# Sixteen batches written out without a loop, with a new order of the steps, in an attention and gate kernel

## The chip, the cores and the metric

The kernel runs on one core of one Trainium2 chip. The metric is the device time of one execution, in microseconds (us). It is stated as the median of several runs; beside it stands one profiled execution, from which every row below comes.

## The reference

For each of 16 batches of 512 tokens with 256 features, two networks read the same normalised tokens, and their product is added to the input:

```python
xn = _layernorm(x)
s = attention(xn)        # "talking heads": 16 heads of 16
g = silu(ffn(xn))        # 2 layers of local attention and a gated feed-forward
return x + s * g

# attention, per batch
logits = einsum(q, k) * SCALE
logits = einsum('bhij,gh->bgij', logits, Wpre)    # mix the heads before the softmax
attn = softmax(logits)
attn = einsum('bhij,gh->bgij', attn, Wpost)       # and after it
out = einsum(attn, v) @ Wout.T + bout

# one of the two layers of ffn, per batch
q, k, v = split(shift_token(x) @ wqkv)            # 8 heads of 64, l2norm, rotary, window 128
x = x + local_attention(q, k, v) @ wo
h = layernorm(shift_token(x)) * lg + lb
a, g = split(h @ w1 + b1)                         # 682 hidden columns each
x = x + (a * gelu(g)) @ w2 + b2
```

All of it is float32. Several products split each operand into a high and a low part and add three products of the parts.

## The kernel before

The work of a batch is cut into 351 steps, named by what they do and by their indices, and every engine goes through the same list and does its own part of each step.

The attention with mixed heads ("talk") has 64 tiles of 8 query rows by 16 heads, which makes 128 rows. `expand` on POOL spreads the queries with the mixing weights (`q_mix`), `part` splits them (ACT makes `q_hi`, POOL `q_lo`), `scores` multiplies on PE, takes the maximum on DVE and the exponential on ACT, and prepares `mixer_n` on DVE. `mix` multiplies `probs` by `mixer_n`, and DVE and ACT take turns at copying its bank M away. After each 8 tiles `values` multiplies by the values in pieces of 32 columns, and after each 16 `project` gives 128 tokens of output.

The gate network ("feed") goes, for each of its two layers, through `x_turn`, 4 windows of `qkv`, `join`, `q_turn` and `k_turn`, then 8 units of `local_scores` (64 rows deep), `weigh`, `p_turn` and `local_values` (64 columns), `out_proj`, then `half_turn`, `shift_turn`, `h_scale`, `h_turn`, 6 chunks of `up` (each with a Gelu on ACT) and 4 of `down`.

`AHEAD` are the steps that prepare the next batch's attention (`norm`, `scale`, `x_turn` 0, `talk_q`, `talk_k`, `talk_v`); they stand late in the list and work on batch b + 1. `BEHIND` are those that finish batch b - 1 (`bound`, four `sigmoid`, `silu`, `gated`, `store`); they stand early in the list. A `sigmoid` is an addition and a reciprocal on DVE.

The place of each step comes from three lists of numbers (`GATE_AT`, `FEED_AT`, `BEHIND_AT`): after how many steps of the talk part it stands. The resulting order is the same for each batch. `Counts.run` writes batch 0 out, then writes one body inside `eng.Fori(1, B)` that each engine repeats 15 times, and then writes `BEHIND` once more for the last batch:

```python
go(AHEAD, 0, True, early=True)
go(order, 0, True)
with eng.Fori(1, B) as b:
    go(order, b, False)
go(BEHIND, B, False)
```

Since the body is one for all, the last pass through it also loads a 17th batch (`x_next` is the input with batch 0 once more behind it) and does `AHEAD` for it, and the weights for a next batch are loaded once more.

`hidden` has 6 chunks of hidden columns; 682 columns leave 42 for the last. `down` multiplies the last chunk with 42 rows (L805):

```python
m = hidden_rows(i)
last = mm(bank[k][:, 0:D], hidden[0:m, i, t * P:(t + 1) * P], w_2[0:m, i, :], ...)
```

`w_2` holds zeros behind its 682nd row. Banks S0, S1, M, V and F0 to F3 are the eight of PSUM; a filling of a bank waits until its last one was emptied.

Of the kernel before, what the change touches and what calls it, by code (L numbers as in the profile page):

```python
# [14 lines left out]
P = 128  # L15
# [9 lines left out]
CT = 8  # L25
# [25 lines left out]
def hidden_rows(c):  # L51
    return min(P, HID - c * P)


# [5 lines left out]
def talk_steps():  # L60

    steps = []
    for n in range(TILES):
        steps.append(("scores", n))
        if n % CT == LAG and n >= CT:
            steps.append(("values", n // CT - 1))
        if n >= LAG:
            steps.append(("mix", n - LAG))
        if n % (2 * CT) == 5 and n >= CT:
            steps.append(("project", n // (2 * CT) - 1))  # L70
    assert LAG == 2
    return steps + [("mix", TILES - 2), ("talk_q",), ("mix", TILES - 1), ("talk_k",), ("values", CHUNKS - 1), ("talk_v",),
                    ("project", TW - 1)]


def feed_steps():

    steps = [("expand", 0)]
    for c in range(TILES // ET):
        steps += [("part", c), ("expand", c + 1)]  # L80
    return steps[:-1]


def gate_steps():

# [33 lines left out]
GATE_AT = [  # L119
# [6 lines left out]
]  # L126
FEED_AT = [
# [49 lines left out]
def gate_network_kernel(nc, a, out):  # L177

    order = step_order()

    filling, fillings = {}, {k: 0 for k in BANKS}
    for step in order:
        for k in banks_of(step):
            fillings[k] += 1
            filling[step, k] = fillings[k]

    early, ahead = {}, {k: 0 for k in BANKS}
    for step in AHEAD:
        for k in banks_of(step):
            ahead[k] += 1  # L190
            early[step, k] = ahead[k]

    with ExitStack() as ctx:
# [118 lines left out]
        filled = {k: sem(f"filled_{k}", fillings[k]) for k in BANKS}  # L312
        emptied = {k: sem(f"emptied_{k}", fillings[k]) for k in BANKS}
# [80 lines left out]
        class Counts:  # L394
# [24 lines left out]
            def run(self, eng, steps):

                def go(list_of_steps, b, first, early=False):
                    for step in list_of_steps:
                        if step[0] not in steps or step in BEHIND and first:
                            continue

                        self.b, self.first = (b + 1, False) if step in AHEAD and not early else (b, first)
                        steps[step[0]](step, *step[1:])
                        self.b, self.first = b, first
                go(AHEAD, 0, True, early=True)
                go(order, 0, True)  # L430
# [1118 lines left out]
```

## Time and profile before

| what | value |
| --- | --- |
| median of 3 runs | 5783.68 us (5781.62 to 5785.23) |
| the profiled execution | 5776.03 us, of which the span from the first to the last instruction is 5774.5 us |
| PE busy | 5549.4 us, 96% of the span |
| DVE busy | 3780.9 us, 65% |
| ACT busy | 2649.4 us, 46% |
| POOL busy | 2645.7 us, 46% |
| mean granted PE clock | 0.986 |

A busy PE means that a matmul was under way. Matmuls overlap, and so the distance from one start to the next says what one costs. Where rows below give a gap before an instruction, it stands in brackets, with what ended it; "issue" stands for a gap in which the engine waited for nothing that the profile shows. The granted clock is a share of the full one, 2.4 GHz; 0.5 is 1.2 GHz.

### The profile page before, as it was taken

The numbers are of one execution on the slowest core, as the hardware profiler recorded it, in microseconds if no ns is written. First come the engines' busy times: TensorE is split into PE (matmuls) and PEld (weight loads), VectorE is DVE, ScalarE is ACT, GpSimd is POOL, SyncE is SP. The second block draws the span as 40 slices with busy tenths as digits, with TensorE's granted clock in tenths as the row PEclk, the third lists the DMA queues.
The fourth block names the chain that finished last, engine by engine and source line by source line (L and its number), as shares of the span: only waits on it lengthen the run. The fifth ranks groups of instructions, "written<-read, shape, count | busy, mean of one in ns | idle before, by whom it ended". The sixth has DMA issues, their size and how long they took to land.

```text
span 5774.5 us, 138883 instructions
## 1 busy us (share of the span) xinstructions
PE 5549.4 (96%) x48336; PEld 4599.6 (80%) x48336; DVE 3780.9 (65%) x9938; ACT 2649.4 (46%) x6527; POOL 2645.7 (46%) x2315
## 2 busy tenths in 40 slices
PE   7999999999999999999999999999999999999998
PEld 5888878788787887878878788787877878778786
DVE  6666766666766667666676666766667676566665
ACT  4444544345443454534445344454444544445443
POOL 4344444444544445444354444544444444445443
PEclk9999999999999999999999999999999999999999
DMA  2211111111101111011110110101111111111111
GB/s 73 88 61 63 37 35 56 42 63 37 60 32 56 49 42 58 28 56 49 47 54 28 56 60 36 53 28 57 59 42 58 39 39 56 42 58 43 35 56 45
DMA packets 52185, 285.49 MB, mean 49 GB/s; under 512 B 5377, under 2 KB 22785, under 8 KB 34177
## 3 DMA queue, kind: packets, MB, share of 16 engines
q1 hardware_dynamic: 40560, 258.59, 12.1%
q0 software_dynamic: 10896, 17.30, 1.6%
q8 instruction: 443, 7.26, 0.5%
q14 instruction: 286, 2.33, 0.1%
HBM read 255.43 MB, written 28.84 MB: 49 GB/s over the span
## 4 chain that ended last, share of the span: by engine, by line
PE 87%; issue 5%; DVE 5%; ACT 1%; POOL 1%; DVEq 0%; SPq 0%; DMA 0%; ACTq 0%; POOLq 0%
PE bank_M L621 15%; PE bank_S L611 8%; PE bank_S L613 7%; PE bank_S L612 7%; PE bank_F L805 6%; PE bank_F L561 5%; PE bank_F L562 5%; PE bank_F L563 5%; PE bank_V L637 4%; PE bank_F L694 4%; PE bank_V L725 4%; PE bank_F L737 4%; PE bank_F L709 4%; PE bank_V L644 2%; PE bank_S L561 1%
## 5 line engine op out<-in xcount | busy, mean ns | idle before, releaser
L1388 POOL TENSOR_TENSOR q_lo<-q_mix,q_hi 128x512 fp32r<-128x512 f32 x512 | 684.4, 1337 | 1613.9 <-ACT q_hi L869 1613.7
L879 ACT ACTIVATE probs<-bank_S,neg_max 128x512 f32<-128x512 f32 x1024 | 701.9, 685 | 1260.5 <-DVE neg_max L1109 1258.6
L621 PEld LDWEIGHTS bank_M<-mixer_n,probs 128*128 128x128 f32 x8192 | 1048.2, 193 | 188.6 <-issue 109.8
L621 PE MATMUL bank_M<-mixer_n,probs 128*128 128x128 f32 x8192 | 1118.2, 280 | 63.7 <-ACT mixed L455 48.4
L1109 DVE TENSOR_REDUCE neg_max<-bank_S 128x1 f32<-128x512 f32 x1024 | 702.3, 686 | 567.2 <-PE bank_S L613 564.1
L611 PE MATMUL bank_S<-k_hi,q_lo 128*128 128x512 f32 x2048 | 898.4, 439 | 5.5 <-POOL q_lo L1388 5.5
L613 PE MATMUL bank_S<-k_hi,q_hi 128*128 128x512 f32 x2048 | 809.6, 395 | 0.0
L612 PE MATMUL bank_S<-k_lo,q_hi 128*128 128x512 f32 x2048 | 808.0, 395 | 0.0
L1382 POOL TENSOR_TENSOR q_mix<-q_rope,w_pre 128x256 f32<-128x256 f32 x1024 | 644.0, 657 | 57.6 <-POOL q_rope L1371 2.4
L932 ACT ACTIVATE l_probs<-l_probs,l_least 128x256 f32<-128x256 f32 (+1 forms) x1024 | 480.5, 471 | 264.4 <-DVE l_least L1198 264.3
L1414 POOL TENSOR_TENSOR l_probs<-l_probs,l_inv 128x1024 f32<-128x1024 f32 (+1 forms) x256 | 430.1, 1680 | 327.2 <-DVE l_inv L1218 327.2
L1399 POOL TENSOR_TENSOR inv_norms<-norms_c,minus_half 128x16 f32<-128x16 f32 x128 | 371.4, 2901 | 381.9 <-DVE norms_c L1152 381.9
L1198 DVE CUSTOM_DVE_ANT_0 l_probs<-bank_F,mask,inv_norms 128x256 f32<-128x256 f32 (+1 forms) x1024 | 401.9, 446 | 133.0 <-issue 131.6
L611 PEld LDWEIGHTS bank_S<-k_hi,q_lo 128*128 128x128 f32 x2048 | 389.5, 190 | 109.1 <-issue 51.1
L613 PEld LDWEIGHTS bank_S<-k_hi,q_hi 128*128 128x128 f32 x2048 | 387.2, 189 | 90.2
L1100 DVE TENSOR_SCALAR mixer_n<-mixer,row_inv 128x128 f32<-128x128 f32 x1024 | 424.1, 414 | 52.7
L869 ACT ACTIVATE q_hi<-q_mix 128x512 fp32r<-128x512 f32 x512 | 320.7, 626 | 264.6 <-POOL q_mix L1382 264.6
L612 PEld LDWEIGHTS bank_S<-k_lo,q_hi 128*128 128x128 f32 x2048 | 391.1, 191 | 50.7
L455 DVE COPY mixed<-bank_M 128x512 f32<-128x512 f32 x512 | 350.3, 684 | 100.5 <-PE bank_M L621 97.7
L1138 DVE TENSOR_TENSOR shared<-bank_F,rot 128x512 f32<-128x512 f32 x512 | 321.9, 683 | 113.9 <-PE bank_F L563 106.4
L805 PE MATMUL bank_F<-w,att 128*128 128x256 f32 (+1 forms) x1536 | 380.7, 392 | 0.0
L1297 DVE SCALAR_TENSOR_TENSOR att<-bank_F,b,shared 128x512 f32<-128x512 f32 x192 | 143.8, 749 | 339.3 <-ACT shared L984 329.0
(143 smaller groups left out, 10210.9 us busy)
## 6 DMA issues: line engine op xcount, KB each, us to landing
w_qkv_hi<-split_qkv SPq DMA_DIRECT2D x31, 1536.0 KB, 6.9
w_qkv_lo<-split_qkv SPq DMA_DIRECT2D x31, 1536.0 KB, 6.6
w_hi<-split SPq DMA_DIRECT2D x31, 1408.0 KB, 6.0
w_lo<-split SPq DMA_DIRECT2D x30, 1408.0 KB, 7.0
w<-in_w SPq DMA_DIRECT2D x33, 768.0 KB, 4.3
w_o<-in_w_o SPq DMA_DIRECT2D x33, 512.0 KB, 5.3
x_in<-in_x_next POOLq DMA_DIRECT2D x17, 512.0 KB, 3.9
out_y<-in_x_next SPq DMA_DIRECT2D x16, 512.0 KB, 7.5
```

Source lines behind the costliest of these rows:

```text
L611: mm(bank[k][:], q_lo[q], k_hi[:, s, :], start=(s == 0), stop=False)
L612: mm(bank[k][:], q_hi[q], k_lo[:, s, :], start=False, stop=False)
L613: last = mm(bank[k][:], q_hi[q], k_hi[:, s, :], start=False, stop=(s == 1))
L621: last = mm(bank["M"][:, j * P:(j + 1) * P], probs[:, n % PB, j * P:(j + 1) * P], mixer_n[:, n % 2, :], start=True, stop=True)
L805: last = mm(bank[k][:, 0:D], hidden[0:m, i, t * P:(t + 1) * P], w_2[0:m, i, :], start=(i == 0), stop=(i == HC - 1))
L879: fn(probs[:, n % PB, :], bank[k][:], ACT.Exp, bias=neg_max[:, n % 2:n % 2 + 1], accum_out=row_sum[:, n % PB:n % PB + 1]).then_inc(emptied ...
L932: fn(l_probs[:, u % LB, j, lo:], l_probs[:, u % LB, j, lo:], ACT.Exp, scale=-1.0, bias=l_least[:, u % 2, j:j + 1], accum_out=l_sum[:, u % ...
L1100: v.tensor_scalar(mixer_n[:, n % 2, :], mixer[:].rearrange("p g i -> p (g i)"), row_inv[:, n % 2:n % 2 + 1], None, ALU.mult).then_inc(mixe ...
L1109: v.tensor_reduce(neg_max[:, n % 2:n % 2 + 1], bank[k][:], AX.X, ALU.max, negate=True)\
L1382: g.tensor_tensor(q_mix[:, s].rearrange("p m (g i) -> p m g i", g=GH), q[:, :, None, :].to_broadcast(shape), w_pre[:, None, :, None].to_br ...
L1388: g.tensor_tensor(q_lo[:, c % QB], q_mix[:], q_hi[:, c % QB].bitcast(F32), ALU.subtract)\
L1414: g.tensor_tensor(l_probs[:, u % LB, :, lo:], l_probs[:, u % LB, :, lo:], l_inv[:, u % 2, :, None].to_broadcast([P, 4, 2 * P - lo]), ALU.m ...
```

## The change

The loop is gone. A function `program()` gives the list of all steps of all batches, each with its batch, and every engine's code is written out from it. Batch 0, the batches 1 to 14 and batch 15 have an order each, which are written out as text, step by step; a step still names the same work, except that `join` and `weigh` now also have their own places against their neighbours. The last order has no `AHEAD`, and its own `BEHIND` steps (`end.`) inside it. Loads of a batch or weights that nobody would use are left out. The waits on banks count fillings through the whole program. `project` also waits until ACT has copied the `values` before it. `down` multiplies 128 rows of the last chunk, and `up` writes 64 rows of it instead of 42 (its other rows meet zeros of `w_2`).

```diff
+ORDER = """
+expand.0 part.0 expand.1 bound qkv.0.0 join.0.0 scores.0 part.1 expand.2 qkv.0.1 scores.1 scores.2 join.0.1 part.2
+q_turn.0.0 expand.3 k_turn.0.0 mix.0 qkv.0.2 scores.3 mix.1 part.3 k_turn.0.1 q_turn.0.1 join.0.2 scores.4 scores.5
+expand.4 mix.2 part.4 qkv.0.3 mix.3 k_turn.0.2 scores.6 mix.4 join.0.3 expand.5 q_turn.0.2 scores.7 scores.8 mix.5
+q_turn.0.3 k_turn.0.3 mix.6 sigmoid.0 part.5 scores.9 mix.7 local_scores.0.0 scores.10 weigh.0.0 scores.11 mix.8
+expand.6 part.6 expand.7 local_scores.0.1 sigmoid.1 part.7 values.0 weigh.0.1 p_turn.0.0 mix.9 local_scores.0.2
+scores.12 expand.8 weigh.0.2 local_values.0.0 mix.10 p_turn.0.1 sigmoid.2 part.8 expand.9 scores.13 mix.11 sigmoid.3
...
+expand.31 scores.57 scores.58 values.6 mix.56 h_scale.1 scores.59 part.31 mix.57 h_turn.1 scores.60 scores.61 norm
+mix.58 up.1.0 scores.62 scale mix.59 up.1.1 up.1.2 mix.60 scores.63 x_turn.0 mix.61 up.1.3 up.1.4 mix.62 up.1.5 mix.63
+talk_q talk_k values.7 down.1.0 down.1.1 talk_v down.1.2 down.1.3 project.3
+"""
...
+LAST_ORDER = """
...
+up.0.1 part.17 mix.27 up.0.2 expand.18 up.0.3 up.0.4 up.0.5 scores.30 mix.28 scores.31 down.0.0 part.18 expand.19
...
+scores.60 mix.58 up.1.0 up.1.1 mix.59 up.1.2 up.1.3 part.31 up.1.4 up.1.5 end.silu scores.61 scores.62 down.1.0
+down.1.1 down.1.2 down.1.3 end.bound scores.63 end.gated end.sigmoid.0 end.store mix.60 mix.61 mix.62 end.sigmoid.1
+mix.63 end.sigmoid.2 values.7 end.sigmoid.3 project.3
+"""
...
+def program():
+
+    end = [("end", *step) for step in BEHIND]
...
+    steps = [(step, 0) for step in AHEAD]
+    for b in range(B - 1):
+        steps += [(step, b + (step in AHEAD)) for step in (step_order() if b else first_order()) if b or step not in BEHIND]
+    return steps + [(step[1:], B) if step[0] == "end" else (step, B - 1) for step in last_order()]
...
             def run(self, eng, steps):
...
-                go(AHEAD, 0, True, early=True)
-                go(order, 0, True)
-                with eng.Fori(1, B) as b:
-                    go(order, b, False)
-                go(BEHIND, B, False)
+                for step, b in steps_of_all:
+                    if step[0] in steps:
+                        self.b, self.first = b, b == 0
                         steps[step[0]](step, *step[1:])
...
             def qkv(step, l, t):
-                if t == TW - 1 and (l or not now.first):
+                if t == TW - 1 and (l or not now.first) and not last(l):
...
             def project(step, t):
                 pe.wait_ge(emptied["V"], now.fill(step, "V") - 1)
+                pe.wait_ge(emptied["V"], now.fill(("values", 2 * t + 1), "V"))
...
                 for i in range(HC):
-                    m = hidden_rows(i)
-                    last = mm(bank[k][:, 0:D], hidden[0:m, i, t * P:(t + 1) * P], w_2[0:m, i, :],
+                    last = mm(bank[k][:, 0:D], hidden[:, i, t * P:(t + 1) * P], w_2[:, i, :],
                               start=(i == 0), stop=(i == HC - 1))
...
-                m, b = hidden_rows(i), BLOCKS - 1 if i == HC - 1 else i
+                m, b = (TAIL_G, BLOCKS - 1) if i == HC - 1 else (P, i)
...
-                if not l:
-
-                    pool.dma_start(x_in[:], a["x_next"][bass.ds(now.b + 1, 1)].rearrange("a p t f -> (a p) t f"))\
-                        .then_inc(x_loaded, 16)
+                if not l and now.b < B - 1:
+
+                    pool.dma_start(x_in[:], a["x"][now.b + 1]).then_inc(x_loaded, 16)
```

## Rows read from the trace of the kernel before

**Rows 1.** The page, part 1: busy time, share of the span, instructions.

```profile
PE 5549.4 (96%) x48336; PEld 4599.6 (80%) x48336; DVE 3780.9 (65%) x9938; ACT 2649.4 (46%) x6527; POOL 2645.7 (46%) x2315
```

**Rows 2.** Waits of PE: total us, times, longest.

```profile
PE bank_M L621 <- ACT mixed L455: 48.4, 15, 3.2
...
PE bank_F L562 <- issue: 28.8, 14, 2.3
PE bank_F L561 <- issue: 27.3, 14, 2.5
```

**Rows 3.** Stretches: the start of the program, and its end behind PE; busy per engine, granted clock.

```profile
0.00:45.00 45.00, 12.42 (x56) 10.49 (x57) 14.74 (x34) 9.57 (x10) 6.68 (x9) 1.00 0.65 232
...
5751.00:5774.50 23.50, 0.00 (x0) 0.00 (x0) 8.86 (x10) 1.06 (x1) 6.03 (x3) 0.61 0.17 22
```

**Rows 4.** Timeline of PE from batch 0 into the first pass.

```profile
416.97 1.89 PE L644 MATMUL bank_V<-w_out,oT 128*128 128x256 f32 x8
...
422.83 0.39 PE L611 MATMUL bank_S<-k_hi,q_lo 128*128 128x512 f32 x1
```

**Rows 5.** Timeline of PE from the sixth pass into the seventh.

```profile
2543.87 1.89 PE L644 MATMUL bank_V<-w_out,oT 128*128 128x256 f32 x8
2547.83 0.79 PE L561 MATMUL bank_F<-w_qkv_hi,xT_hi 128*128 128x512 f32 x1 [2.08 <-issue]
...
2556.36 0.39 PE L611 MATMUL bank_S<-k_hi,q_lo 128*128 128x512 f32 x1
```

**Rows 6.** Stretches: a place in the seventh pass, and the way into it; columns as above.

```profile
2589.90:2599.00 9.10, 5.88 (x23) 4.88 (x24) 7.44 (x21) 3.07 (x9) 3.00 (x4) 0.62 0.00 1
2544.70:2557.80 13.10, 9.01 (x30) 6.79 (x30) 4.38 (x8) 2.31 (x4) 4.07 (x6) 0.74 0.02 6
```

**Rows 7.** Timeline of PE and its weight loads in the last batch.

```profile
5740.18 6.03 PE L805 MATMUL bank_F<-w,att 128*128 128x256 f32 x24
...
5742.53 0.29 PEld L805 LDWEIGHTS bank_F<-w,att 42*128 42x128 f32 x2 [0.33 <-issue]
...
5746.14 0.39 PE L561 MATMUL bank_S<-w_v_hi,xT_hi 128*128 128x256 f32 x1
...
5749.09 1.89 PE L644 MATMUL bank_V<-w_out,oT 128*128 128x256 f32 x8
```

**Rows 8.** Groups of instructions of PE and POOL: busy us, mean ns of one, idle before.

```profile
L644 PE MATMUL bank_V<-w_out,oT 128*128 128x256 f32 x512 | 121.0, 379 | 0.0
...
L1399 POOL TENSOR_TENSOR inv_norms<-norms_c,minus_half 128x16 f32<-128x16 f32 x128 | 371.4, 2901 | 381.9 <-DVE norms_c L1152 381.9
```

**Rows 9.** Timeline of PE: the `scores` right behind a `local_scores`.

```profile
2604.15 0.50 PE L611 MATMUL bank_S<-k_hi,q_lo 128*128 128x512 f32 x1
2604.49 0.40 PE L612 MATMUL bank_S<-k_lo,q_hi 128*128 128x512 f32 x1
```

**Rows 10.** Timeline of DVE, then of PE, in the seventh pass.

```profile
2587.46 1.75 DVE L1322 RECIPROCAL x_mid<-x_mid 128x256 f32<-128x256 f32 x1
...
2589.39 1.75 DVE L1322 RECIPROCAL x_mid<-x_mid 128x256 f32<-128x256 f32 x1
2591.06 0.63 DVE L1109 TENSOR_REDUCE neg_max<-bank_S 128x1 f32<-128x512 f32 x1
...
2593.12 2.05 PE L621 MATMUL bank_M<-mixer_n,probs 128*128 128x128 f32 x8 [3.23 <-ACT mixed L455]
```

**Rows 11.** Timeline of PE at the same place in the second pass.

```profile
815.18 1.13 PE L621 MATMUL bank_M<-mixer_n,probs 128*128 128x128 f32 x8 [3.23 <-ACT mixed L455]
...
821.21 0.72 PE L694 MATMUL bank_F<-att 64*128 64x128 f32 x8 [1.78 <-DVE l_least L1198]
```

**Rows 12.** Timeline of ACT in the last batch.

```profile
5740.31 0.39 ACT L895 ACTIVATE oT<-bank_V 128x256 f32<-128x256 f32 x1 [4.05 <-PE bank_V L637]
5740.72 1.28 ACT L989 ACT_TABLE_LOAD   x1
```

**Rows 13.** Timeline of DVE and POOL behind PE's last matmul.

```profile
5751.48 0.69 DVE L1315 TENSOR_SCALAR x_mid<-x_tok 128x1024 f32<-128x1024 f32 x1
...
5766.38 1.35 POOL L1442 DMA_DIRECT2D out_y<-s_tok  x1 [0.30 <-POOL s_tok L1437]
```

**Rows 14.** Timeline of PE: one `values`.

```profile
406.13 1.99 PE L637 MATMUL bank_V<-mixed,v_heads 128*32 128x64 f32 x128
```

More of the change, by code:

```diff
@@ L60, in talk_steps, with value_steps @@
 def talk_steps():
+    assert LAG == 2
     steps = []
[L63 to L73, printed above, removed]
+    for n in range(TILES + LAG):
+        steps += [("scores", n)] * (n < TILES) + [("mix", n - LAG)] * (n >= LAG)
+    return steps
+def value_steps():
+    steps = []
+    for c in range(CHUNKS):
+        steps += [("values", c)] + [("project", c // 2)] * (c % 2)
+    return steps
 def feed_steps():
@@ L81, in feed_steps, with join_steps @@
     return steps[:-1]
+def join_steps():
+    steps = []
+    for l in range(LAYERS):
+        steps += [("join", l, t) for t in range(TW)] + [("weigh", l, u) for u in range(TW * QUADS)]
+    return steps
 def gate_steps():
@@ new lines @@
+x_turn.1 mix.31 scores.33 part.18 qkv.1.0 values.3 join.1.0 qkv.1.1 k_turn.1.0 join.1.1 expand.19 q_turn.1.0 mix.32
+scores.34 scores.35 qkv.1.2 k_turn.1.1 q_turn.1.1 part.19 expand.20 mix.33 join.1.2 qkv.1.3 mix.34 scores.36 join.1.3
+q_turn.1.2 part.20 k_turn.1.2 scores.37 scores.38 q_turn.1.3 mix.35 k_turn.1.3 scores.39 expand.21 mix.36
+local_scores.1.0 project.1 weigh.1.0 mix.37 part.21 scores.40 expand.22 mix.38 part.22 p_turn.1.0 local_scores.1.1
+scores.41 expand.23 mix.39 part.23 weigh.1.1 local_values.1.0 local_scores.1.2 scores.42 values.4 local_scores.1.3
@@ new lines @@
+"""
+FIRST_ORDER = """
+expand.0 part.0 expand.1 qkv.0.0 join.0.0 part.1 scores.0 expand.2 qkv.0.1 join.0.1 scores.1 k_turn.0.0 part.2
+q_turn.0.0 expand.3 qkv.0.2 mix.0 scores.2 k_turn.0.1 join.0.2 bound scores.3 part.3 expand.4 q_turn.0.1 mix.1 qkv.0.3
+mix.2 scores.4 scores.5 silu q_turn.0.2 k_turn.0.2 part.4 sigmoid.0 mix.3 join.0.3 expand.5 scores.6 mix.4 scores.7
+k_turn.0.3 q_turn.0.3 sigmoid.1 part.5 mix.5 local_scores.0.0 mix.6 scores.8 local_scores.0.1 expand.6 part.6 scores.9
+mix.7 weigh.0.0 scores.10 local_scores.0.2 values.0 p_turn.0.0 weigh.0.1 mix.8 scores.11 expand.7 weigh.0.2
@@ new lines @@
+x_turn.1 mix.31 part.19 scores.33 qkv.1.0 values.3 join.1.0 qkv.1.1 k_turn.1.0 mix.32 q_turn.1.0 expand.20 join.1.1
+scores.34 qkv.1.2 mix.33 part.20 join.1.2 store q_turn.1.1 expand.21 k_turn.1.1 scores.35 qkv.1.3 sigmoid.3 mix.34
+scores.36 join.1.3 k_turn.1.2 q_turn.1.2 part.21 scores.37 scores.38 expand.22 q_turn.1.3 mix.35 k_turn.1.3 scores.39
+mix.36 local_scores.1.0 part.22 project.1 weigh.1.0 mix.37 scores.40 mix.38 local_scores.1.1 scores.41 expand.23
+mix.39 p_turn.1.0 weigh.1.1 local_scores.1.2 part.23 values.4 mix.40 scores.42 scores.43 p_turn.1.1 weigh.1.2
@@ new lines @@
+part.28 mix.50 out_proj.1.2 local_values.1.6 p_turn.1.7 expand.29 mix.51 local_values.1.7 scores.53 part.29
+out_proj.1.3 scores.54 mix.52 scores.55 expand.30 part.30 expand.31 mix.53 half_turn.1 scores.56 mix.54 shift_turn.1
+project.2 mix.55 scores.57 scores.58 h_scale.1 values.6 mix.56 scores.59 mix.57 h_turn.1 scores.60 scores.61 norm
+mix.58 up.1.0 part.31 scale up.1.1 mix.59 up.1.2 mix.60 scores.62 scores.63 x_turn.0 mix.61 up.1.3 up.1.4 mix.62
+up.1.5 talk_q mix.63 talk_k down.1.0 talk_v down.1.1 down.1.2 values.7 down.1.3 project.3
@@ new lines @@
+down.0.1 down.0.2 down.0.3 mix.29 x_turn.1 mix.30 scores.32 scores.33 mix.31 qkv.1.0 join.1.0 values.3 qkv.1.1
+k_turn.1.0 scores.34 join.1.1 part.19 mix.32 q_turn.1.0 qkv.1.2 mix.33 scores.35 scores.36 q_turn.1.1 join.1.2
+expand.20 mix.34 k_turn.1.1 part.20 qkv.1.3 mix.35 q_turn.1.2 scores.37 scores.38 k_turn.1.2 join.1.3 mix.36 scores.39
+scores.40 expand.21 mix.37 q_turn.1.3 k_turn.1.3 part.21 scores.41 mix.38 local_scores.1.0 project.1 expand.22 part.22
+mix.39 local_scores.1.1 weigh.1.0 expand.23 part.23 weigh.1.1 scores.42 mix.40 local_scores.1.2 values.4 scores.43
@@ L524, in up @@
                     spill_1(l)
-                if i == HC - 1 and (l or not now.first):
+                if i == HC - 1 and (l or not now.first) and not last(l):
                     k, = banks_of(step)
@@ L1543 @@
          for k, v in arrays.items()}
-    a["x"] = a["x_next"]
     out = nc.dram_tensor("out_y", (B, N, D), F32, kind="ExternalOutput").ap()
```

158 lines of the change are left out of this document (92 added, 66 removed), and 9 rows, old and new, of tables (FEED_AT, GATE_AT).

## Prediction

> **What bounds the kernel now.** The first thing to read is the busy share of each engine [rows 1]. PE works in 5549.4 of 5774.5 us, DVE in 65% of them, ACT and POOL in 46%. So PE sets the time, and a change is worth what it takes from PE: matmul time, gaps, or clock. PE is idle for 225.1 us in all. The second view is its waits, which say where [rows 2]: 56.1 us go to two gaps marked "issue" that come 14 times each, and 48.4 us to one `mix` that waits 15 times. The stretches give two more [rows 3]: 45.0 - 12.4 = 32.6 us before the first `qkv`, and 23.5 us behind the last matmul. What is left over is 225.1 - 56.1 - 48.4 - 32.6 - 23.5 = 64.5 us in small waits, 4.0 us a batch. The third view is the timeline of PE at those places, since a gap is followed by slow matmuls, and the distance between starts shows what busy time hides.
>
> **The loop's end.** Between batch 0 and the first pass nothing branches back: from the last `project` (416.97) to the first `scores` (422.83) PE needs 5.86 us [rows 4]. Between the sixth pass and the seventh the same instructions need 2556.36 - 2543.87 = 12.49 us, with a gap of 2.08 us that waits for nothing [rows 5]; the second gap is as long, 28.8/14 = 2.06 us [rows 2]. The other 2.6 us are clock: 0.74 was granted over that stretch, so for a time after the idle gaps PE runs at 1.2 instead of 2.4 GHz [rows 6]. The back edge thus costs 12.49 - 5.86 = 6.6 us here. The 14 back edges have 56.1 us of gaps, 4.0 each, against 4.1 here, and I take 6.4 each: **14 x 6.4 = 90 us**. If the clock came down for another reason and stayed down, the gaps alone, 56 us, would be gained; more than 93 (14 x 6.6) I cannot see.
>
> The crossing from batch 0 into the first pass is straight code and has no such gap. The Trainium skill ("Runtime: NRT & Kernel Launch", Instruction fetch mechanics) says the same: instructions are fetched ahead in sequence only, a taken branch to a far target must wait, and straight code hides its fetching. By that rule all 90 us go, and 15 times as many written-out instructions add no gap; the trace agrees as far as batch 0 shows it.
>
> **The last chunk of `down`.** Two `down` steps take 5746.14 - 5740.18 = 5.96 us, 2.98 each for 12 matmuls [rows 7]. Full-height matmuls of 256 columns lie (1.89 - 0.38) / 7 = 0.216 us apart: that is `project`'s row [rows 7], where a single one lasts 379 ns [rows 8]. Twelve of them are 2.59 us. The 0.39 us of difference lies at the 42-row loads, before which the load path stands idle for 0.33 us [rows 7]. With 128 rows no such edge is left, and rows cost no columns. There are 16 x 2 x 4 = 128 of these steps, all on PE's path: **128 x 0.39 = 50 us**. Where a `down` has a neighbour with another shape, one of its two edges stays; in the new orders no `down` is followed by `values` in batches 1 to 14, so I take off nothing. The 64 rows that `up` writes instead of 42 run side by side and cost nothing on DVE or ACT.
>
> **Fewer changes of shape.** The same edge stands wherever PE goes between full height and width and `local_scores` (64 rows), `local_values` (64 columns) or `values` (32 columns). Half of 0.39 is 0.2 us an edge; what can be seen outside the odd step alone is 0.34 - 0.23 = 0.11 us in the first distance behind `local_scores` [rows 9]. Counting neighbours in PE's order, the old body has 76 edges, the order of batches 1 to 14 has 69, the first 66 and the last 71. That is 14 x 7 + 10 + 5 = 113 edges: at 0.2 **23 us**, at 0.11 it would be 12.
>
> **The four sigmoids.** In each pass DVE does sigmoids 1 and 2 back to back. Its next maximum, at 2591.06, comes at least 3.6 us after 2587.46, and the `mix` that follows starts 3.23 us late [rows 10]. That is the 48.4 us in the waits (the waiting `mix` is put down to ACT, but ACT waits for DVE's maximum). Batch 0 has no sigmoids, and no such wait. In the seventh pass the clock then falls (0.62 over 9.1 us [rows 6]), and the eight matmuls that end the gap take 2.05 us instead of 1.13; in the second it stays up, but PE meets a next wait of 1.78 us 6 us later [rows 11]. So one pass loses 3.23 + 1.78 = 5.0 us, another 3.23 plus up to 2.7 of clock; I take 5.5. The new order sets `sigmoid.0` behind `mix.6`, `.1` behind the second `local_scores`, and the last two with a `scores` and a `mix` between them. I added up DVE's and PE's work along both lists. With the old one DVE falls 5.3 us behind PE at the first `local_scores`, with the new one never more than 3.5 in that part. Two tiles of PE's work (2 x 2.3 us) lie between a `scores` and its `mix`, and maximum, exponential and scaling need about 2, so a lag up to some 3 us is hidden. So the wait goes: **15 x 5.5 = 82 us**. Bounds: nothing, if the lag merely moves, and 88.
>
> **The other waits.** 4.0 us a batch. Some come from places that the new order changes (`mix.61` before `x_turn` 0, `scores.60`), and 1.4 us a batch would be a third of them: 15 x 1.4 = 21 us. Against it stands ACT: the old list changes between Exp and Gelu four times a batch, the new one eight times, since `scores.62` and `scores.63` stand among the `up` steps. Each change is a table load of 1.28 us, which starts as soon as the activation before it ends [rows 12]. ACT is busy 46%, so 14 x 4 x 1.28 = 72 us of work are hidden nearly everywhere. Where they might show is `up.1.4`, which needs the bank that ACT and DVE empty after `x_turn` 0: adding up from `up.1.0`, I find it 0.7 us late. 14 x 0.7 = 10 us. Together **10 us**, between -72 (all loads exposed) and +64 (no wait left).
>
> The Trainium skill ("ScalarE: Activation LUTs", What ACT_TABLE_LOAD costs) prices a change of table at about 2.66 us, of which a drain is half. The trace shows 1.28 and no drain in front of the load, and I go by the trace.
>
> **The last batch.** It has no `AHEAD`: `talk_q` and `talk_k` are 24 matmuls of 0.24 us (of the 5.86 us of [rows 4], 8 x 0.216 = 1.7 are `project`'s at most, and 18 matmuls of 512 columns share the other 4.2), 5.7 us, `x_turn` (8 of 0.11) 0.9. `talk_v` lay behind `down` and is counted in what follows. Now the end: the last `down` ends at 5746.14 [rows 7], and 28.4 us later all is over. In the new order `bound` follows it at once (0.7 us for the addition), the chain from `bound` to the end stays 5774.5 - 5751.48 = 23.0 us [rows 13], its last part being the store, 8.1 us. Up to 2.6 us of DVE's work for `scores.63` and two `mix` comes between the sigmoids: 26.3 instead of 28.4, 2 us gained. Under the chain lies now what PE did before it: `scores.63` 1.4 us, four `mix` of 0.9, `values` 1.9 [rows 14] = 6.9 us. Sum: 5.7 + 0.9 + 6.9 + 2 = **16 us**, between 9 (nothing hidden) and 19.
>
> Batch 0 keeps its waits for the splitting of the weights. The loads left out are off the path (DMA waits do not appear in rows 2). `join` and `weigh` move against their neighbours on POOL, priced under the rivals.
>
> **Sum.** 90 + 50 + 23 + 82 + 10 + 16 = 271 us. The profiled execution took 5776.0 us, so 5505 us. The median of the runs shown lies 7.7 us above that execution; 5505 + 7.7 gives **5513 us**, -4.7%.
>
> **Rivals.**
> 1. No wait is left in the batches: the 64.5 us of small waits go instead of 10. 5513 - 54 = 5459 us. For it: DVE, ACT and POOL have room. Against it: DVE still falls behind at times.
> 2. The reordering brings nothing: the lag of DVE moves elsewhere and makes an equal wait, so the 82 and the 10 fail. 5513 + 92 = 5605 us. For it: DVE's work in the first 60 us of a batch is the same (some 92% of PE's), and taking 6.4 us of stops out of PE gives it less time to catch up.
> 3. The table loads are exposed: 72 us instead of 10 hidden in the sum, 5513 + 62 = 5575 us. For it: `part` and `scores` wait for ACT in order. Against it: ACT's 46%.
> 4. Slower than before: POOL. In the new order `part.1` stands behind `join.0.0`, and so behind a power of 2.9 us [rows 8] that waits for all of `qkv.0.0` on DVE; the old list had three parts done before it. I get `q_lo` for `scores.2` 0.2 us before PE wants it. [...] To end on the other side this must cost 271/14 = 19 us in each batch, while only one power and one product (4 us) lie in front of it. 3 in 100.
>
> **Chances and range.** The sum 0.62, no waits left 0.12, reordering in vain 0.13, tables 0.08, slower 0.03, no change 0.02. The likeliest one's own range is 5470 to 5555: shape edges at 0.11 and 3 us of waits a batch more on one side, 3 us less on the other. The range that holds 8 in 10 is 5445 to 5590: it takes in the first and the third rival, and part of the second. Differences below 0.2% could not be told from none by a measurement of this kernel. Faster by more than that: 0.95; within: 0.02; slower: 0.03.
>
> **What would show it.** Right: PE's waits for "issue" are gone, and no matmul at 1.2 GHz is seen at batch starts; the 42-row form is gone and `down` steps are 2.59 us; the 3.2 us wait before a `mix` is gone; the batches are some 337 to 340 us apart, against 355.5 (5332 us for 15); ACT has about 60 more table loads; the mean granted clock is above 0.99. Wrong: a new wait that comes 14 times, above all at `scores` for `q_lo` or at `mix`; or gaps for "issue" spread over the straight code.

## The result, and the profile after

| | before | after |
| --- | --- | --- |
| median of 4 runs | 5782.65 us (5775.81 to 5785.23) | 5510.11 us (5509.82 to 5510.46) |
| profiled span | 5774.5 us | 5508.7 us |
| mean granted PE clock | 0.986 | 0.997 |

The ratio is 0.953, with a 95% interval of 0.9514 to 0.9547: the changed kernel takes 4.7% less. 5513 was predicted.

The page of the changed kernel, part 1, which answers to [rows 1]:

```profile
PE 5403.8 (98%) x48280; PEld 4601.9 (84%) x48280; DVE 3794.9 (69%) x9913; ACT 2710.1 (49%) x6581; POOL 2647.8 (48%) x2308
```

PE is idle for 104.9 us instead of 225.1, so 120 of the 266 us of span were gaps. The other 146 are busy time: 56 fewer matmuls, but above all matmuls that no longer run at 1.2 GHz, no longer stretch over a change of shape, and `down` without its odd chunk. Waits of PE (total us, times, longest), for [rows 2]:

```profile
PE bank_F L657 <- DVE x_in L1138: 32.1, 1, 32.1
PE bank_S L696 <- POOL q_lo L1473: 21.7, 16, 5.5
PE bank_V L811 <- ACT pT L1026: 8.7, 14, 0.9
PE bank_V L762 <- POOL shared L1491: 8.2, 17, 0.5
PE bank_M L706 <- ACT mixed L537: 7.5, 18, 1.6
...
PE bank_V L722 <- issue: 3.4, 8, 0.9
```

Both rows of 14 gaps for "issue" are gone, and so is the wait of 3.2 us before a `mix`. What is left at the top is the start of the program (once) and a wait of `scores` for `q_lo`: 5.5 us once in batch 0, which the kernel before had too, and new 16.0 us in the 14 steady batches, as batches 1 to 14 are called here. The last row is small, but it belongs to the signs that the prediction gave: `values`, which is 128 short matmuls, stops 8 times in its middle for "issue", where it did so 3 times for 0.8 us in all before. Stretches (busy time of each engine, granted clock), for [rows 3] and [rows 6]:

```profile
0.00:45.00 45.00, 11.41 (x53) 9.68 (x54) 14.38 (x34) 9.57 (x10) 6.33 (x9) 1.00 0.65 232
...
400.00:5160.00 4760.00, 4717.22 (x42339) 4019.94 (x42338) 3311.99 (x8665) 2365.83 (x5758) 2318.27 (x2021) 1.00 0.14 49
```

The clock is granted in full over the steady batches. The timeline of PE where one batch passes into the next, for [rows 5]:

```profile
2438.01 5.34 PE L890 MATMUL bank_F<-w,att 128*128 128x256 f32 x24
2443.19 1.89 PE L730 MATMUL bank_V<-w_out,oT 128*128 128x256 f32 x8
2444.73 0.58 PE L646 MATMUL bank_F<-w_qkv_hi,xT_hi 128*128 128x512 f32 x1
...
2449.00 0.39 PE L696 MATMUL bank_S<-k_hi,q_lo 128*128 128x512 f32 x1
```

From `project` to the first `scores` it now takes 2449.00 - 2443.19 = 5.81 us, as in batch 0 before [rows 4], and not 12.49. Two `down` steps take 5.18 us, 2.59 each, instead of 5.96 [rows 7]. From start to start the steady batches are 339.2 us apart, against 355.5.

### The profile page after: what moved, and what is told of

It is laid out like the page before. It is cut to its first block and busy times, and to the rows that moved or that the text cites. A ratio compares the mean times of both kernels' runs of the same rounds, so it can differ in the third digit from the quotient of the medians.

```text
span 5508.7 us, 130052 instructions
## 1 busy us (share of the span) xinstructions
PE 5403.8 (98%) x48280; PEld 4601.9 (84%) x48280; DVE 3794.9 (69%) x9913; ACT 2710.1 (49%) x6581; POOL 2647.8 (48%) x2308
## 5 line engine op out<-in xcount | busy, mean ns | idle before, releaser
L706 PE MATMUL bank_M<-mixer_n,probs 128*128 128x128 f32 x8192 | 1092.9, 276 | 12.8 <-ACT mixed L537 7.5
L696 PE MATMUL bank_S<-k_hi,q_lo 128*128 128x512 f32 x2048 | 877.4, 428 | 21.7 <-POOL q_lo L1473 21.7
L1484 POOL TENSOR_TENSOR inv_norms<-norms_c,minus_half 128x16 f32<-128x16 f32 x128 | 402.9, 3147 | 334.6 <-DVE norms_c L1237 332.8
L1185 DVE TENSOR_SCALAR mixer_n<-mixer,row_inv 128x128 f32<-128x128 f32 x1024 | 431.6, 421 | 169.0 <-PE bank_M L706 57.7
L537 ACT COPY mixed<-bank_M 128x512 f32<-128x512 f32 x512 | 296.9, 580 | 142.1 <-PE bank_M L706 83.1
```

The costliest lines, as they stand in the source:

```text
L537: copy(mixed[:, :, :, m * RI:(m + 1) * RI], bank["M"][:].rearrange("p (j g i) -> p j g i", j=TW, g=GH)).then_inc(emptied["M"], 1)
L696: mm(bank[k][:], q_lo[q], k_hi[:, s, :], start=(s == 0), stop=False)
L706: last = mm(bank["M"][:, j * P:(j + 1) * P], probs[:, n % PB, j * P:(j + 1) * P], mixer_n[:, n % 2, :], start=True, stop=True)
L1185: v.tensor_scalar(mixer_n[:, n % 2, :], mixer[:].rearrange("p g i -> p (g i)"), row_inv[:, n % 2:n % 2 + 1], None, ALU.mult).then_inc(mixe ...
```

## The experiments

Twelve kernels ran. Batch lengths are distances between first `qkv` matmuls, a mean over batches 1 to 14; the last batch runs from its first `qkv` matmul to the end. In the sets of runs below the kernel before had medians of 5775.7 to 5778.6 us, so spans and batch lengths compare better than differences of medians.

### The parts one by one

**a: whole rows alone.** In the kernel before, `down` takes 128 rows and `up` writes 64.

```diff
-                    m = hidden_rows(i)
-                    last = mm(bank[k][:, 0:D], hidden[0:m, i, t * P:(t + 1) * P], w_2[0:m, i, :],
+                    last = mm(bank[k][:, 0:D], hidden[:, i, t * P:(t + 1) * P], w_2[:, i, :],
```

> The kernel before (loop and old order), with the last chunk of down alone multiplied in 128 rows. Theory (each down loses 0.39 us at its 42-row matmuls, all on PE's path): 5783 - 50 = 5733 us, and down steps of 2.59 us instead of 2.98. Rival (the freed time is lost again in waits of the old order, since PE reaches them earlier): 5758 us or more, and longer waits of PE.

Measured: 5735.68 us, ratio 0.9929 (0.9912 to 0.9946), 40.0 us less; its span is 42.4 us shorter. A `down` step got 0.37 us shorter in the traces (2.93 to 2.56 in the mean), 48 us in all; the rest came back in waits: the two rows for "issue" grew from 56.1 to 60.2 us.

**b: no loop, and nothing else.** All three orders are the old list, the last one without `AHEAD`; `down` keeps its 42 rows.

```diff
-                with eng.Fori(1, B) as b:
-                    go(order, b, False)
+                for step, b in steps_of_all:
```

> The kernel after with the old order in every batch and 42 rows in down: the loop alone is gone, and with it the 17th AHEAD. Theory (a back edge costs 6.4 us of gap and low clock, 14 of them, and 10 us of PE work of the unneeded AHEAD): 5783 - 100 = 5683 us, no wait for issue, PE's clock up at the starts of batches. Rival 1 (gaps go, the clock stays down): 5717 us. Rival 2 (straight code is fetched no faster, the gaps spread over it): about 5770 us, with issue gaps at other places.

Measured: 5687.19 us, ratio 0.9844 (0.9828 to 0.9861), 88.5 us less. Neither row for "issue" of [rows 2] is there any more. The wait of the `mix` is, and larger: 54.3 us in 15 places instead of 48.4. The timeline of PE where batch 6 passes into batch 7, which answers to [rows 5]:

```profile
2522.18 1.89 PE L730 MATMUL bank_V<-w_out,oT 128*128 128x256 f32 x8
2523.71 0.58 PE L646 MATMUL bank_F<-w_qkv_hi,xT_hi 128*128 128x512 f32 x1
...
2528.04 0.39 PE L696 MATMUL bank_S<-k_hi,q_lo 128*128 128x512 f32 x1
```

These are 5.86 us, and so it is at every crossing of b, within 0.01. In the kernel before the 14 crossings take 9.76 to 13.34 us, 12.15 in the mean, and so b gains 88 us at the crossings alone. Its batches, however, are only 5.3 us shorter (355.6 to 350.25), 75 us in all; the last batch is 13.9 us shorter. The rest is not waits: without the two rows for "issue" PE is idle for 169.0 us before, and for 167.9 in b. It is clock. From the waiting `mix` to 12 us behind its start the granted clock was 1.00 in 4 of the 14 steady batches before, and 0.74 to 0.86 in the others; in b it is 0.73 to 0.86 in all 14. What the lower clock takes in the part around that `mix` (20 to 80 us into a batch) grows by that from 1.7 to 2.7 us a batch, as an estimate from the granted clock.

**c: b with whole rows**, so that only the new order is missing.

```diff
-                    last = mm(bank[k][:, 0:D], hidden[0:m, i, t * P:(t + 1) * P], w_2[0:m, i, :],
+                    last = mm(bank[k][:, 0:D], hidden[:, i, t * P:(t + 1) * P], w_2[:, i, :],
```

> As the kernel without the loop and with the old order, and 128 rows in down. Theory (the two parts add): 5633 us. What is then missing to the kernel after, 5510 us, is the new order: 123 us. Rival (they share a wait): 5645 us or more.

Measured: 5643.32 us, ratio 0.9767 (0.9751 to 0.9784), 132.4 us less; against 40.0 + 88.5 = 128.5 for the two alone, they add up. Its waits of PE, and the seventh batch's:

```profile
PE bank_M L706 <- ACT mixed L537: 54.4, 15, 3.6
PE bank_F L657 <- DVE x_in L1138: 40.9, 16, 31.2
PE bank_M L706 <- DVE mixed L537: 13.8, 31, 1.4
```

```profile
2546.24 1.13 PE L706 MATMUL bank_M<-mixer_n,probs 128*128 128x128 f32 x8 [3.63 <-ACT mixed L537]
```

So the order of the steps carries 5643.32 - 5510.11 = 133 us, half of the whole gain.

The straight code has gaps for "issue" of its own, at other places. In c PE stops in the middle of a `values`:

```profile
2258.63 1.86 PE L722 MATMUL bank_V<-mixed,v_heads 128*32 128x64 f32 x115
2262.44 0.42 PE L722 MATMUL bank_V<-mixed,v_heads 128*32 128x64 f32 x13 [1.95 <-issue]
```

There are five such gaps at `values` in b (5.7 us) and in c (7.1 us), and the eight in the changed kernel (3.4 us). That is b's second rival, but small: it expected some 5770 us. No run shows what these gaps wait for.

### Where the order's gain comes from

**d: the old order with its sigmoids spread out.** Against c, each `sigmoid` has other steps between itself and the next. All four also come later, and `silu` and `gated` move behind them:

```diff
-mix.1 part.3 expand.4 join.0.3 scores.4 sigmoid.0 mix.2 q_turn.0.3 scores.5 part.4 mix.3 sigmoid.1 sigmoid.2 expand.5
-scores.6 k_turn.0.3 mix.4 scores.7 part.5 mix.5 sigmoid.3 local_scores.0.0 scores.8 mix.6 local_scores.0.1 scores.9
+mix.1 part.3 expand.4 join.0.3 scores.4 mix.2 q_turn.0.3 scores.5 part.4 mix.3 expand.5 scores.6 k_turn.0.3 mix.4
+scores.7 part.5 mix.5 sigmoid.0 local_scores.0.0 scores.8 mix.6 local_scores.0.1 sigmoid.1 scores.9 expand.6 weigh.0.0
+mix.7 sigmoid.2 local_scores.0.2 weigh.0.1 scores.10 values.0 p_turn.0.0 mix.8 sigmoid.3 silu gated part.6
```

> As the last one, with the four sigmoids alone moved apart in the old order: behind mix.5, the second local_scores, mix.7 and mix.8, with silu and gated behind them. Theory (two sigmoids back to back make DVE 3.2 us late for a mix, and with what follows that costs 5.5 us in each of 15 batches): 5633 - 82 = 5551 us, and the 48 us wait of mix for ACT is gone. Rival (DVE's work is the same, its lag comes out at another step): about 5633 us, with a new wait that comes 15 times.

Measured: 5646.89 us, ratio 0.9778 (0.9762 to 0.9794): no gain over c. The waits of PE show where the time went:

```profile
PE bank_S L696 <- POOL q_lo L1473: 31.7, 16, 5.5
PE bank_F L780 <- DVE l_least L1283: 22.3, 29, 1.0
PE bank_V L811 <- ACT pT L1026: 20.5, 15, 1.4
```

The large wait at the `mix` is gone, and three others, 74.5 us, stand in its place (in c the first is 5.5, the second 2.5 us, and the third is not there). The expected 5551 us was missed, and the rival, the lag coming out at another step, held. Not all of it comes out at DVE itself. Before the 2.23 us wait for `q_lo` in batch 6, POOL does the two products of `gated`, which wait for the last sigmoid:

```profile
2209.43 2.39 POOL L1516 TENSOR_TENSOR x_mid<-x_mid,x_tok 128x1024 f32<-128x1024 f32 x1 [2.48 <-DVE x_mid L1407]
2211.96 2.35 POOL L1521 TENSOR_TENSOR s_tok<-s_tok,x_mid 128x1024 f32<-128x1024 f32 x1
2214.27 1.26 POOL L1473 TENSOR_TENSOR q_lo<-q_mix,q_hi 128x512 fp32r<-128x512 f32 x1
```

So this one way of spreading the sigmoids in the old order moves the wait; whether another would do better was not tried.

**e: the new order with its sigmoids squeezed together** as in the old list.

```diff
-expand.4 mix.2 part.4 qkv.0.3 mix.3 k_turn.0.2 scores.6 mix.4 join.0.3 expand.5 q_turn.0.2 scores.7 scores.8 mix.5
-q_turn.0.3 k_turn.0.3 mix.6 sigmoid.0 part.5 scores.9 mix.7 local_scores.0.0 scores.10 weigh.0.0 scores.11 mix.8
+expand.4 mix.2 part.4 qkv.0.3 mix.3 k_turn.0.2 scores.6 sigmoid.0 mix.4 sigmoid.1 sigmoid.2 join.0.3 expand.5
+q_turn.0.2 scores.7 scores.8 mix.5 q_turn.0.3 k_turn.0.3 mix.6 sigmoid.3 part.5 scores.9 mix.7 local_scores.0.0
```

> The kernel after with the sigmoids of batches 1 to 14 moved back early: behind scores.6, two together behind mix.4, the last behind mix.6. Theory (DVE has no slack there, two in a row make a maximum late): some 3 to 5 us a batch more, 5510 + 14 x 4 = 5566 us, with a wait of mix of 2 to 3 us, 14 times. Rival (the new order has slack enough elsewhere; the old wait came from something else): 5510 to 5520 us.

Measured: 5610.06 us, ratio 0.9713 (0.9698 to 0.9728), 100 us more than the changed kernel, 7.2 us a batch, where 3 to 5 were expected. The wait comes 14 times, as expected, but at a `q_turn` (L762) and not at a `mix`. The wait and the stretch around it:

```profile
PE bank_F L762 <- DVE shared L1251: 44.6, 14, 3.2
```

```profile
2526.00:2536.00 10.00, 8.20 (x40) 6.73 (x41) 7.98 (x17) 3.94 (x9) 3.49 (x4) 0.66 0.01 2
```

Over the 10 us around such a wait the granted clock is 0.66. Of the 100 us, 59 are idle time of PE (163.7 us instead of 104.8; 45 of them this wait, the rest waits that grew elsewhere), and 40 are busy time for the same number of matmuls (5443.5 instead of 5403.8 us). Of the two placements tried, neither was enough alone: the spread sigmoids in the old list, and the squeezed ones in the new.

**k and l: the sigmoids' work taken out**, in the old order (k, on c) and in the new one (l, on the changed kernel).

```diff
-                fn(x_mid[:], x_mid[:], ACT.Exp, scale=-1.0).then_inc(exp_done, 1)
+                fn(x_mid[:], x_mid[:], ACT.Copy, scale=-1.0).then_inc(exp_done, 1)
...
-                v.reciprocal(x_mid[:, t, :], x_mid[:, t, :]).then_inc(sig_done, 1)
+                v.reciprocal(x_mid[:, t, 0:1], x_mid[:, t, 0:1]).then_inc(sig_done, 1)
```

> The kernel without the loop and with whole rows in down, but with the old order of steps, in which each sigmoid's reciprocal covers one column instead of the whole tile and the exponential ahead of it is a plain copy (so the sigmoids' values are left out; about 1.6 us of VectorE work four times a batch is gone). Theory, that VectorE's lag behind the sigmoids is what costs 6.7 us a batch in the old order: 5643 less 15 x 6.7 = 100, about 5543 us, and the wait of the mixes for ScalarE (54 us in 15 places) gone. Rival, that the lag has another source: 5620 us or more, with that wait still there.

> The changed kernel with the same cut: each sigmoid's reciprocal covers one column, its exponential is a plain copy (the sigmoids' values are left out). Theory, that the new order already absorbs the sigmoids: within some 10 us of the changed kernel's 5510 us, 5495 to 5510. Rival, that the new order only spreads the sigmoids' price over many small waits: tens of us less, 5480 or below.

Measured: k 5563.57 us, ratio 0.9629 (0.9614 to 0.9644), 79.8 us less than c where 100 were expected; its batches went from 347.53 to 342.55 us, 5.0 each. The wait of the `mix` fell as k's row shows:

```profile
PE bank_M L706 <- ACT mixed L537: 9.3, 15, 0.6
```

l 5504.63 us, ratio 0.9529 (0.9514 to 0.9543), 5.5 us less than the changed kernel; its batches stay 339.2 us apart, so that in the steady batches of the new order the sigmoids cost nothing that can be seen. In the profiles the difference lies in batch 0, which has no sigmoids (5.3 us, scatter), and in the last batch (2.0). So the sigmoids cost 79.8 us in the old order and at most 5.5 in the new one: 74 of the 133 us or a little more. The other 59 stand between k and l, where no sigmoid plays a part: 14 x 3.35 = 47 in the steady batches (342.55 and 339.20 us), 12.6 in batch 0 (371.3 and 358.7), and under 2 in the last. The 14 steady batches of k, then of l:

```profile
414.55:5210.17 4795.62, 4740.45 (x42170) 3984.75 (x42169) 3239.81 (x8652) 2301.20 (x5698) 2321.16 (x2017) 1.00 0.14 49
```

```profile
403.20:5152.01 4748.81, 4706.29 (x42171) 4010.40 (x42169) 3223.57 (x8652) 2363.19 (x5754) 2312.57 (x2016) 1.00 0.14 49
```

The clock is the full one in both, and the matmuls are the same. PE's busy time falls by 34 us, so its matmuls lie closer together, and its idle time by 13.

### The table loads

**g: the `up` steps of layer 1 kept together**, `scores.62` and `scores.63` before them.

```diff
-mix.58 up.1.0 scores.62 scale mix.59 up.1.1 up.1.2 mix.60 scores.63 x_turn.0 mix.61 up.1.3 up.1.4 mix.62 up.1.5 mix.63
+mix.58 scale mix.59 scores.62 mix.60 scores.63 up.1.0 up.1.1 up.1.2 x_turn.0 mix.61 up.1.3 up.1.4 mix.62 up.1.5 mix.63
```

> The kernel after with scores.62 and scores.63 of batches 1 to 14 set before up.1.0, so that ACT changes its table 4 times a batch instead of 6 for the second layer's part (28 loads of 1.28 us less or more gone). Theory (the loads are hidden): the same within 0.3%, 5500 to 5525 us; all that can change is small waits from the closer row of scores and mix. Rival (exposed loads): 5510 - 14 x 2 x 2.6 = 5440 us.

Measured: 5593.33 us, ratio 0.9682 (0.9667 to 0.9697), 83 us more. Both expectations missed, although 56 loads are gone (69 instead of 125) and not 28. The waits of the `mix` for DVE and ACT grew to 30.7 and 30.3 us and `x_turn` now waits 24.2: from `mix.58` to `scores.63` no PE work of the feed part stands between the tiles any more. It suggests that the `up` steps are cover for the tiles; of the loads it tells nothing, since the edit moved both.

**h: four more loads in each steady batch**, behind the exponentials of `scores.62` and `scores.63`, and the order left alone.

```diff
+                if n >= TILES - 2 and 0 < now.b < B - 1:
+                    j = 4 * now.b + 2 * (n % 2)
+                    fn(spare[:, j:j + 1], b_qk[:, 0:1], ACT.Gelu)
+                    fn(spare[:, j + 1:j + 2], b_qk[:, 0:1], ACT.Exp)
```

> The changed kernel with four more table loads in each of batches 1 to 14 where the ups lie: a one-column Gelu and a one-column Exp on ScalarE behind the exponentials of scores.62 and of scores.63 (extra work, nothing left out); some 56 more loads of 1.28 us, 72 us of ScalarE in all, and about 0.9 us a batch of small instructions. Theory, that ScalarE has room there and the loads lie beside TensorE's work: 5510 to 5520 us. Rival, that table loads at the ups are exposed: up to 72 us more by the loads alone and 84 with the small instructions, 5580 to 5594 us.

Measured: 5540.57 us, ratio 0.9588 (0.9573 to 0.9603), 30.5 us more, between the two expectations. Two new waits of PE, 14 times each:

```profile
PE bank_F L647 <- DVE xT_lo L1150: 15.7, 14, 1.1
PE bank_F L658 <- DVE att L1387: 14.1, 14, 1.3
```

```profile
2423.30 1.28 ACT L969 ACT_TABLE_LOAD   x1
2424.59 0.20 ACT L969 ACTIVATE spare<-b_qk 128x1 f32<-128x1 f32 x1
2424.80 1.28 ACT L970 ACT_TABLE_LOAD   x1
2426.09 0.20 ACT L970 ACTIVATE spare<-b_qk 128x1 f32<-128x1 f32 x1
2426.20 1.06 ACT L932 ACTIVATE xT_hi<-bank_F 128x512 fp32r<-128x512 f32 x2
```

At each of the two places 3.0 us of ACT went in and about 1.1 us of PE came out. The changed kernel itself has no wait at `up.1.3` or `up.1.4`. So its own loads are hidden; the room left at each place is, as an estimate from these numbers, 3.0 - 1.1 = 1.9 us, and no more.

### The end, and the new wait

**i: the last batch in the steady order**, without `AHEAD`, its `end.` steps behind everything.

```diff
-expand.0 part.0 bound expand.1 qkv.0.0 scores.0 join.0.0 part.1 expand.2 scores.1 qkv.0.1 scores.2 q_turn.0.0 part.2
...
+down.1.1 down.1.2 down.1.3 project.3 end.bound end.sigmoid.0 end.sigmoid.1 end.sigmoid.2 end.sigmoid.3 end.silu
+end.gated end.store
```

> The kernel after, where the last batch has the order of the others without AHEAD, and its own BEHIND steps stand behind everything. Theory (the order of the last batch puts 6.9 us of PE's work under the chain of sigmoids and stores and lets bound start earlier): 6 to 9 us more, 5518 us. Rival (the end costs the same, since the chain is shared with DVE's other work): 5510 us.

Measured: 5511.32 us, ratio 0.9543 (0.953 to 0.9556), 1.2 us more, where 6 to 9 were expected; that is too little to be told from none. Within the profiled last batch it is 3.8 us (354.3 against 350.5). PE behind the last `down` steps, changed kernel:

```profile
5471.78 10.52 PE L890 MATMUL bank_F<-w,att 128*128 128x256 f32 x48
...
5486.14 1.13 PE L706 MATMUL bank_M<-mixer_n,probs 128*128 128x128 f32 x8 [1.57 <-ACT mixed L537]
5488.15 1.13 PE L706 MATMUL bank_M<-mixer_n,probs 128*128 128x128 f32 x8 [0.88 <-DVE mixed L537]
```

```profile
5483.07 0.69 DVE L1400 TENSOR_SCALAR x_mid<-x_tok 128x1024 f32<-128x1024 f32 x1 [0.30 <-DVE x_tok L1391]
...
5501.03 1.34 POOL L1526 DMA_DIRECT2D out_y<-s_tok  x1 [0.30 <-POOL s_tok L1521]
```

and in i:

```profile
5474.40 10.63 PE L890 MATMUL bank_F<-w,att 128*128 128x256 f32 x48
5484.86 1.89 PE L730 MATMUL bank_V<-w_out,oT 128*128 128x256 f32 x8
```

The last order moves its last `down` forward by 5.7 us within the batch, but the chain behind it takes 5508.7 - 5482.3 = 26.4 us against 5509.5 - 5485.0 = 24.5. DVE needs 10.9 us for the four sigmoids, with the `scores` and `mix` work between them, and 7.9 us in i, where they stand alone.

**f: `part.1` before `qkv.0.0`** in all three orders.

```diff
-expand.0 part.0 expand.1 bound qkv.0.0 join.0.0 scores.0 part.1 expand.2 qkv.0.1 scores.1 scores.2 join.0.1 part.2
+expand.0 part.0 expand.1 part.1 bound qkv.0.0 join.0.0 scores.0 expand.2 qkv.0.1 scores.1 scores.2 join.0.1 part.2
```

> The kernel after with part.1 set ahead of bound and qkv.0.0 in each order, so that POOL makes this q_lo before the power and the product of join. Theory (PE waits 1.14 us for it 14 times, and 5.5 us in batch 0 for the first): 14 x 1.1 = 16 us less, 5494 us. Rival (the wait passes on to the next q_lo or to a window of qkv that now comes later): 5505 to 5512 us.

Measured: 5489.54 us, ratio 0.9504 (0.9491 to 0.9517), 20.6 us less than the changed kernel, a little more than the 16 expected. The batches are 338.0 us apart, which is 17 us for the 14, and of the wait for `q_lo` only batch 0's is left:

```profile
PE bank_S L696 <- POOL q_lo L1473: 5.5, 1, 5.5
```

**m: f with four more steps moved**, each of which waits in every steady batch.

```diff
-q_turn.0.3 k_turn.0.3 mix.6 sigmoid.0 part.5 scores.9 mix.7 local_scores.0.0 scores.10 weigh.0.0 scores.11 mix.8
-expand.6 part.6 expand.7 local_scores.0.1 sigmoid.1 part.7 values.0 weigh.0.1 p_turn.0.0 mix.9 local_scores.0.2
-scores.12 expand.8 weigh.0.2 local_values.0.0 mix.10 p_turn.0.1 sigmoid.2 part.8 expand.9 scores.13 mix.11 sigmoid.3
+q_turn.0.3 mix.6 k_turn.0.3 sigmoid.0 part.5 scores.9 mix.7 local_scores.0.0 scores.10 weigh.0.0 scores.11 mix.8
+expand.6 part.6 expand.7 local_scores.0.1 sigmoid.1 part.7 values.0 weigh.0.1 mix.9 p_turn.0.0 local_scores.0.2
+scores.12 expand.8 weigh.0.2 mix.10 local_values.0.0 p_turn.0.1 sigmoid.2 part.8 expand.9 scores.13 mix.11 sigmoid.3
...
-x_turn.1 mix.31 scores.33 part.18 qkv.1.0 values.3 join.1.0 qkv.1.1 k_turn.1.0 join.1.1 expand.19 q_turn.1.0 mix.32
+x_turn.1 mix.31 scores.33 part.18 qkv.1.0 values.3 join.1.0 qkv.1.1 join.1.1 expand.19 q_turn.1.0 k_turn.1.0 mix.32
```

> The kernel in which the part of the local attention's norm on GpSimd is issued earlier (5489.5 us), with four more steps moved in batches 1 to 14: local_values.0.0 behind mix.10, p_turn.0.0 behind mix.9, k_turn.0.3 behind mix.6, k_turn.1.0 behind q_turn.1.0. These are the steps that wait longest in each steady batch, some 1.5 us together of what moving can reach. Theory, that each wait ends on work that is only issued too close: 14 x 1.5 = 21 us less, about 5469 us. Rival, that the waits pass on to the next step, since the engine named there is busy throughout: 5485 to 5492 us.

Measured: 5490.48 us, ratio 0.9502 (0.9489 to 0.9515), the same as f. Its waits:

```profile
PE bank_M L706 <- ACT mixed L537: 15.6, 18, 1.6
PE bank_M L706 <- DVE mixed L537: 10.0, 16, 0.9
PE bank_F L795 <- POOL l_probs L1499: 6.7, 14, 0.7
```

The wait for `pT` (8.7 us) is gone and that for POOL's `shared` fell from 7.9 to 1.3 us, but the two rows of the `mix` went from 7.4 and 3.9 us to 15.6 and 10.0, with 6.7 for `l_probs` beside them: 15 us out, 21 in. The rival, that the waits pass on to the next step, was right.

## Why the prediction was right, point by point

The time came out as forecast, and the experiments show each large term; the reason given for one of them, the order, was only half right. That the sum is within 3 us of the measurement is in part luck, since its errors point both ways.

- **Back edges (90 us), with the last batch's missing `AHEAD` (6.6 us in the sum; 10 with `talk_v`, as b's expectation has it).** b was expected to gain 100 us and gained 88.5. The mechanism is shown: the gaps and the slow clock go with the loop, and at the crossings themselves the term is right (88 us). No batch's start has a gap in the straight code. The Trainium skill's rule ("Runtime: NRT & Kernel Launch", Instruction fetch mechanics) says that straight code hides its fetching, and the trace agrees there; at `values` some gaps for "issue" remain, 3.4 us in the changed kernel. What went wrong is that the time gained at the crossings did not all reach the end: the 14 batches got 75 us shorter and not 88, since the clock now came down behind the waiting `mix` in every batch and not in ten of 14. The sum had no term for that.
- **`down` (50 us).** The steps themselves gave 48 us; 40 to 44 reached the end (a alone, and c against b), because part of what PE saves is waited for elsewhere.
- **The order (82 + 23 + 10, and 9 of the last batch's 16, together 124 us).** Measured 133. The largest term, the sigmoids, is 79.8 - 5.5 = 74 us, where 82 stood. The reason given was only half right. By the sum along the lists the new order would never let DVE fall over 3.5 us behind in that part; the lag itself was not measured, but no wait for it is left there. The reason named the sigmoids' spacing. d and e show that this spacing alone is not it: spread out in the old list they gain nothing, squeezed in the new one they cost 100 us. The second rival's mechanism was thus real for d, and not for the change.
- **Shapes, other waits and the last batch (42 us).** 59 us, of which 47 in the steady batches: 34 of busy time and 13 of waits, by the stretches of k and l. The sum had 14 x 7 edges x 0.2 = 20 us of shapes there, and so this term was too small, or the matmuls came closer for another reason as well. No experiment separates them. In the changed kernel a `scores` step takes 1.37 us at the shortest, 1.50 behind a `local_scores`, and 1.58 between a `local_scores` and a `values`, which speaks for 0.1 to 0.2 us a change. Batch 0 was said to keep its waits, but its order gained too: it takes 371.3 to 371.6 us in the three profiles with the old order and whole rows (c, d, k), and 358.7 to 364.0 in six with the new one (the changed kernel, e, g, h, i, l). The six run the same batch 0, and so single profiles scatter by 5 us there.
- **The last batch.** The chain behind the last `down` came out as forecast (26.3 said, 26.4 measured). What the forecast missed is that the plain end's chain would have been 24.5 and not the 28.4 of [rows 7], which still had `talk_v` in it: the last order brings 1 to 4 us, not 9.
- **Table loads (10 us lost at `up.1.4`).** There are 60 more, as forecast, 125 in all, and no wait at `up.1.4`. The third rival fell: h shows that even four more a batch cost 30.5 of 84 us.
- **POOL (the fourth rival).** Its place was right, its size small. `q_lo` for `scores.2` was to come 0.2 us early and came 1.14 us late, 14 times; f took it away and gained 20.6 us. Of the 1.34 us of error, 1.02 are a power that took 3.92 us instead of 2.90 (below).

The sum agrees better than its terms: 7 us of the total are the kernel before itself, whose median was 5782.65 us here and 5775.7 beside a, b and c. From there it is 88.5 + 43.9 + 133.2 = 265.6 us: the back edges and `down` brought less than was said, the order more.

## What to carry to other kernels

Where one engine sets the time, what counts of a second one is how far it falls behind where its work is dense: cut its work to nothing in both orders and the difference of the two gains is what the order hides (79.8 against 5.5 us). Moving the work alone or the list around it alone gave nothing here (d), or cost 100 us (e). And when every remaining wait is of some 1 us or less, look for a step behind a slow one in its own queue (`part.1`, 20.6 us); four moves that only shifted distances gave nothing. And time gained at one place does not all reach the end: 88 us at the crossings became 75 us of shorter batches, because the clock was lower at another place.

## What was not expected of the hardware

**A power on POOL takes longer when a product on DVE began just before it.** Timelines of POOL and of DVE in the changed kernel:

```profile
2450.83 3.92 POOL L1484 TENSOR_TENSOR inv_norms<-norms_c,minus_half 128x16 f32<-128x16 f32 x1 [9.13 <-DVE norms_c L1237]
2454.83 1.05 POOL L1491 TENSOR_TENSOR shared<-shared,inv_norms 128x512 f32<-128x512 f32 x1
2455.83 1.26 POOL L1473 TENSOR_TENSOR q_lo<-q_mix,q_hi 128x512 fp32r<-128x512 f32 x1
...
2458.41 2.90 POOL L1484 TENSOR_TENSOR inv_norms<-norms_c,minus_half 128x16 f32<-128x16 f32 x1
```

```profile
2450.76 1.23 DVE L1251 TENSOR_TENSOR shared<-shared 128x1024 f32<-128x1024 f32 x1
...
2460.20 1.23 DVE L1251 TENSOR_TENSOR shared<-shared 128x1024 f32<-128x1024 f32 x1 [0.20 <-issue]
```

The first power starts 0.07 us after DVE's product and takes 3.92 us; the second has the product begin 1.79 us into it, and takes 2.90. The whole trace follows that. 31 of its 128 powers began while this product ran, 30 of them 0.07 or 0.08 us and one 0.17 us behind it, and these 31 take 3.83 to 3.92 us; the other 97 take 2.90 to 2.99. In the kernel before no power began so, and none took over 2.92. The excess of 1.02 us is nearly the 1.16 us that the product still had to run. The Trainium skill ("SBUF — State Buffer", SBUF: two separate sides) calls the port pair that these two engines share an exclusive lock that whoever starts first keeps for its whole instruction, while the other is blocked. The trace agrees where the product came first. It does not where the power did: the 91 products that began inside a power take 1.21 to 1.23 us, as the 6 do that met none, and so a lock held to the power's end is not seen. No experiment here changed which one starts first.

**A wait also costs clock.** In the squeezed order e the 3.2 us waits sum up to 44.6 us and the kernel is 100 us longer, 40 us of it busy time: the clock was 0.66 over the 10 us around such a wait. In the changed kernel, whose steady waits are 1.15 us or less, it was 1.00 over the steady batches.
